# Second-norm tiles turned in the router's PSUM bank; first-norm tiles keep the turn bank

## What is computed

```python
y = einsum('nsi,oi->nso', patchify(x), tok_W) + tok_b
h = layernorm(y) * ln_w + ln_b
# attention: first norm, then q, k, v; all fake-quantised
a = norm(h)
q, k, v = split(a @ Wqkv.T)                  # 12 heads of 16, clipped to -4..3
p = quant(q @ k.T / 196)                    # clipped to 8 levels from 0 up, no softmax
h = h + quant(p @ v) @ Wproj.T + bproj
# experts: second norm, then router and experts
f = norm(h)
logits = (f @ enc_w + enc_b) @ sw_w + sw_b   # 8 experts
prob = max(softmax(logits)); onehot = one_hot(argmax(logits))
g = gelu(f @ w1[e] + b1[e]) for the chosen e
out = h + prob * (g @ w2[e] + b2[e])
```

## Time and profile before

| | us |
|---|---|
| median of 3 runs | 1179.12 |
| lowest, highest | 1174.66, 1179.33 |
| the profiled execution | 1175.08 |
| its span in the trace | 1173.3 |
| TensorE busy | 1064.0 (91%) |
| TensorE weight loads | 865.9 (74%) |
| VectorE busy | 864.6 (74%) |
| ScalarE busy | 702.7 (60%) |
| GpSimd busy | 619.2 (53%) |

### The profile page before, as it was taken

How to read it: one execution, slowest core, us unless ns; L and a number is a source line. 1 busy time by engine, 2 the same in 40 slices (tenths; PEclk the granted TensorE clock), 3 DMA queues, 4 the chain that set the end, 5 groups by cost and what they waited for, 6 DMA issues and landing times. The chain is left out here.

```text
span 1173.3 us, 26470 instructions
## 1 busy us (share of the span) xinstructions
PE 1064.0 (91%) x8646; PEld 865.9 (74%) x8646; DVE 864.6 (74%) x2976; ACT 702.7 (60%) x1586; POOL 619.2 (53%) x1016
## 2 busy tenths in 40 slices
PE   4788998999999999999999999999999999999987
PEld 4566777877778777777877777787777778777666
DVE  4587677777877878787777778777777877878673
ACT  1356656665675657666665666666666666666551
POOL 3444563737556373755627366462746646374433
PEclk8887999999999999999999999999999999999889
DMA  7120111111111111111112021121202111000000
GB/s 229 36 60 24 49 53 41 51 32 51 43 44 56 42 50 34 51 40 41 59 34 60 23 63 40 40 60 34 60 22 63 40 39 60 10 11 13 8 16 22
DMA packets 33517, 52.80 MB, mean 45 GB/s; under 512 B 5077, under 2 KB 18150, under 8 KB 33382
## 3 DMA queue, kind: packets, MB, share of 16 engines
q1 hardware_dynamic: 33382, 51.10, 14.8%
HBM read 41.45 MB, written 9.63 MB: 44 GB/s over the span
## 5 line engine op out<-in xcount | busy, mean ns | idle before, releaser
L829 ACT ACTIVATE relu<-scores_ps,c_prob 98x784 uint8<-98x784 f32 x384 | 348.5, 908 | 108.6 <-PE scores_ps L624 83.2
L553 PE MATMUL embed_ps<-we,x_sb 128*112 128x192 f32 x1344 | 303.2, 340 | 22.5 <-ACT y L798 13.7
L912 POOL TENSOR_TENSOR ve<-mv,const_sb 112x1 f32<-112x1 f32 x336 | 74.1, 221 | 375.4 <-DVE mv L1274 373.7
L915 POOL TENSOR_TENSOR rs<-ve,const_sb 112x1 f32<-112x1 f32 x336 | 224.8, 669 | 26.5
L553 PEld LDWEIGHTS embed_ps<-we,x_sb 128*112 128x112 f32 x1344 | 208.1, 180 | 38.5 <-issue 17.0
L1119 DVE TENSOR_SCALAR prob<-relu 98x784 uint8<-98x784 uint8 x384 | 219.4, 572 | 13.1 <-ACT relu L829 4.9
L925 POOL TENSOR_TENSOR expd<-econst,below 112x8 f32<-112x8 f32 x112 | 190.8, 1743 | 25.3 <-DVE below L1197 25.3
L1080 DVE TENSOR_SCALAR xn<-h,mv,rs 112x192 f32<-112x192 f32 x224 | 93.7, 424 | 46.6 <-POOL rs L915 44.8
L930 POOL TENSOR_TENSOR m<-n,lnw 112x192 f32<-112x192 f32 x112 | 67.1, 599 | 105.0 <-ACT n L806 104.8
L819 ACT ACTIVATE a_hi<-turn_ps 128x112 fp32r<-128x112 f32 x112 | 29.5, 264 | 141.7 <-PE turn_ps L571 141.0
L570 PE MATMUL turn_ps<-const_sb,xn 112*128 112x112 f32 x224 | 69.3, 309 | 45.1 <-DVE xn L1080 24.2
(11 more groups left out here) (168 smaller groups left out, 2528.7 us busy)
## 6 DMA issues: line engine op xcount, KB each, us to landing
x_sb<-in_x SPq DMA_DIRECT2D x112, 336.0 KB, 2.9
out<-out_sb SPq DMA_DIRECT2D x112, 84.0 KB, 1.7
we<-in_tok_w SPq DMA_DIRECT2D x1, 576.0 KB, 3.9
w_sb<-in_w SPq DMA_DIRECT2D x1, 384.0 KB, 4.4
const_sb<-in_const SPq DMA_DIRECT2D x1, 377.0 KB
raw_q_a<-in_w_qkv SPq DMA_DIRECT2D x1, 288.0 KB
raw_q_b<-in_w_qkv SPq DMA_DIRECT2D x2, 144.0 KB
raw_a<-in_w SPq DMA_DIRECT2D x1, 256.0 KB, 4.3
```

The source lines that it names most:

```text
L553: pe.matmul(dst, x_sb[:, t, j], we[:, j], start=j == 0, stop=False)
L829: act.activation(relu8[:, u % 2], scores_ps[0:KEYS, :, 0:2 * SEQ], ACT.Relu, scale=c_prob[0:KEYS, :]).then_inc(act_relu, 1)
L912: pool.tensor_tensor(ve[:, t], mv[:, t, 1:2], const_sb[0:TT, C_EPS:C_EPS + 1], ALU.add).then_inc(ve_sem, 1)
L915: pool.tensor_tensor(rs[:, t], ve[:, t], const_sb[0:TT, C_HALFNEG:C_HALFNEG + 1], ALU.pow).then_inc(rs_sem, 1)
```

## The change

Second-norm tiles are turned into `route_ps` instead of `turn_ps`; `turn_bank(k)` picks the bank in `turn`, `high` and `low`. The first-norm turns keep `turn_ps`, and wait only for `low` of the first-norm turn before, in this pass or the last. The second-norm turns become users of the router's bank: `ROUTED` gets seven more entries, which wait with `empty` for the user before and are waited for by the user behind, through `dve_lo`. Since entries are sorted by slot, fractions give the order inside a slot as TensorE runs it: turn +0.1, `up` +0 or +0.3 (`up_place`), `route` +0.4, spread +0.5. No instruction is added, dropped or moved in any engine's order.

```diff
--- before.py
+++ after.py
@@ -382,6 +382,10 @@
             TURNS += [(1, t) for t in at(TURN2, s)] + [(2, t) for t in at(TURN3, s)]
             TURNS += [(3, t) for t in at(TURN3, s + SLOTS)]
 
+        def up_place(slot):
+
+            return slot if slot <= EMBED_END[-1] else slot + 0.3
+
         class Turns:
 
 
@@ -414,9 +418,10 @@
         PROJECTED = [(s, 2, dve_h1, NT, t + 1) for t, s in enumerate(PROJ) if s < SLOTS]
         PROJECTED += [(s - SLOTS, 3, dve_h1, NT, t + 1) for t, s in enumerate(PROJ) if s >= SLOTS]
         PROJECTED += [(s, 3, result, NT, t + 1) for t, s in enumerate(DOWN) if t % 2 == 0]
-        ROUTED = [(s, 3, choose, CHOICES, STEPS_A_CHOICE * n + 2) for n, s in enumerate(ROUTE)]
-        ROUTED += [(s, 3, spread_out, 2, n + 1) for n, s in enumerate(SPREAD)]
-        ROUTED += [(s, 3, gelu_out, 8, n + 1) for n, s in enumerate(UP) if n % 2]
+        ROUTED = [(s + 0.4, 3, choose, CHOICES, STEPS_A_CHOICE * n + 2) for n, s in enumerate(ROUTE)]
+        ROUTED += [(s + 0.5, 3, spread_out, 2, n + 1) for n, s in enumerate(SPREAD)]
+        ROUTED += [(up_place(s), 3, gelu_out, 8, n + 1) for n, s in enumerate(UP) if n % 2]
+        ROUTED += [(TURN3[t] % SLOTS + 0.1, k, dve_lo, None, n) for n, (k, t) in enumerate(TURNS) if k != 1]
 
         def empty(eng, users, groups, slot):
 
@@ -433,8 +438,13 @@
                     if isinstance(loop, int) and number < 0:
                         return
                 _, stage, signal, per_group, k = users[n]
+                if groups[stage - 1] is not None and signal is dve_lo:
+                    return wait(eng, dve_lo, turns.before(groups, k + 1))
                 if groups[stage - 1] is not None:
                     return wait(eng, signal, groups[stage - 1].count(per_group, k))
+
+        def turn_bank(k):
+            return turn_ps if k == 1 else route_ps
 
         block = ctx.enter_context(nc.Block())
 
@@ -565,10 +575,17 @@
                 src, made = (xn2, dve_xn2) if k == 1 else (xn3, dve_xn3)
 
                 pe.wait_ge(made, g.count(NT, t + 1))
-                wait(pe, dve_lo, turns.before(groups, n))
+                if k == 1:
+                    m = max(range(n - len(TURNS), n), key=lambda m: (TURNS[m][0] == 1, m))
+                    i = g.offset - (m < 0)
+                    if i >= 0:
+                        wait(pe, dve_lo, turns.before(stages(g.loop, i, i % 2), m % len(TURNS) + 1))
+                else:
+                    empty(pe, ROUTED, groups, TURN3[t] % SLOTS + 0.1)
+                bank = turn_bank(k)
                 rows = src[:, (g.parity + t) % 2]
-                pe.transpose(turn_ps[:, 0:TT], rows[:, 0:128], ident)
-                pe.transpose(turn_ps[0:LO, TT:2 * TT], rows[:, 128:EMBED], ident).then_inc(turned, 1)
+                pe.transpose(bank[:, 0:TT], rows[:, 0:128], ident)
+                pe.transpose(bank[0:LO, TT:2 * TT], rows[:, 128:EMBED], ident).then_inc(turned, 1)
 
             def rows(g, m, half):
 
@@ -661,7 +678,7 @@
                 last.then_inc(projected, 1)
 
             def route(groups, g, part):
-                empty(pe, ROUTED, groups, ROUTE[part])
+                empty(pe, ROUTED, groups, ROUTE[part] + 0.4)
                 need_split3(g, PARTS[part][-1] + 1)
                 for n, t in enumerate(PARTS[part]):
                     cols = slice(TT * t, TT * (t + 1))
@@ -692,7 +709,7 @@
             def up(groups, g, n):
                 part, m = divmod(n, FC)
                 bank, users = (wide_ps, WIDE) if n % 2 == 0 else (route_ps, ROUTED)
-                empty(pe, users, groups, UP[n])
+                empty(pe, users, groups, UP[n] if n % 2 == 0 else up_place(UP[n]))
                 if m == 0:
 
                     pe.wait_ge(spread_out, g.count(2, part + 1))
@@ -816,10 +833,10 @@
                 act.wait_ge(turned, turns.before(groups, n) + 1)
                 if t == 0:
                     reads_done(act, g, k)
-                act.activation(hi[:, g.parity, cols], turn_ps[:, 0:TT], ACT.Copy)
-                last = act.activation(both[0:LO, g.parity, cols], turn_ps[0:LO, TT:2 * TT], ACT.Copy)
+                act.activation(hi[:, g.parity, cols], turn_bank(k)[:, 0:TT], ACT.Copy)
+                last = act.activation(both[0:LO, g.parity, cols], turn_bank(k)[0:LO, TT:2 * TT], ACT.Copy)
                 if k != 1:
-                    last = act.activation(f_c[0:LO, g.parity, cols], turn_ps[0:LO, TT:2 * TT], ACT.Copy)
+                    last = act.activation(f_c[0:LO, g.parity, cols], turn_bank(k)[0:LO, TT:2 * TT], ACT.Copy)
                 last.then_inc(act_hi, 1)
 
             def relu(g, u):
@@ -1106,9 +1123,9 @@
                 hi, lo, both = (a_hi, a_lo, a_b) if k == 1 else (f_hi, f_lo, f_b)
                 cols = slice(TT * t, TT * (t + 1))
                 dve.wait_ge(act_hi, turns.before(groups, n) + 1)
-                dve.tensor_tensor(lo[:, g.parity, cols], turn_ps[:, 0:TT],
+                dve.tensor_tensor(lo[:, g.parity, cols], turn_bank(k)[:, 0:TT],
                                   hi[:, g.parity, cols].bitcast(f32), ALU.subtract)
-                dve.tensor_tensor(both[LO:128, g.parity, cols], turn_ps[0:LO, TT:2 * TT],
+                dve.tensor_tensor(both[LO:128, g.parity, cols], turn_bank(k)[0:LO, TT:2 * TT],
                                   both[0:LO, g.parity, cols].bitcast(f32), ALU.subtract).then_inc(dve_lo, 1)
 
             def quantise(g, u):
```

## The result

The changed kernel takes 1254.93 us as the median of four runs (1253.94 to 1256.71), against 1177.7 us for the kernel before, now with a fourth run of it (1174.66 to 1179.33). The ratio is 1.066, with a 95% interval of 1.063 to 1.069. The direction was right; the time lies 10 us above the forecast range.

A forecast was written before the change was run, and what follows sets the result against it. TensorE, busy 91% of the span in one fixed order, was taken to bound the kernel. 1175.1 profiled + 39.7 for stalls less gain + 13 for the clock = 1227.8, stated as 1228 us, range 1205 to 1245.

The forecast's parts named there:

- The removed waits: Slots 21 and 23: first-norm turns no longer wait for f_b, 18.3 us in all, 1.21 us a pass.
- The two stalls: New TensorE waits: router in slot 2 for tile 4, 2.30 us; expert product in slot 9 for tile 6, 1.32.
- the gain: Slots 21 and 23: idle time saved at first-norm turns, 0.33 + 0.88 = 1.21 us a pass.
- the sum: Steady passes without the clock: 2.30 + 1.32 - 1.21 = 2.41 us each; with passes 1, 16 and 17, +39.7 us.
- the third case: Slot 2's stall mostly swallowed because VectorE sets slots 4 to 6: 1195 us, chance 0.08.
- the three falls of the one before: Clock falls to half in passes 3, 8 and 13, slots 21 to 22, of the kernel before; 1.3 us each.
- The clock: Behind slot 2: half-clock falls in some 13 of 14 steady passes, where 3 had one; 10 x 1.3 = +13 us.
- The case with two stretches a pass: Two half-clock stretches each pass, at slots 2 and 9 or one that lasts: +36 us, 1251 us, chance 0.07.

The follow-up runs named there:

- the kernel with tiles 0 to 3: Changed kernel, but only second-norm tiles 0 to 3 use the router's bank; tiles 4, 5, 6 return to the turn bank: 1161.96 us, ratio 0.990.
- the kernel with tile 4 back: Changed kernel with tile 4 alone returned to the turn bank, removing the router's wait in slot 2: 1184.09 us, ratio 1.008.
- the one with slot 2 filled: Changed kernel plus ten unread products, 448 columns wide, ahead of the router's wait in slot 2: 1224.13 us, ratio 1.042.
- the kernel with all waits filled: Changed kernel plus unread wide products ahead of three waits: ten in slot 2, six in slot 9, four in slot 20: 1210.73 us median, 1206.66 profiled.
- with narrow products: Changed kernel plus twenty unread products, 16 columns wide, ahead of the router's wait in slot 2: 1259.05 us, ratio 1.072.
- with tile 6 back: Changed kernel with tile 6 alone returned to the turn bank, removing the expert product's wait in slot 9: 1237.56 us, ratio 1.054.
- with the wait alone: Kernel before, no tile changing bank, with only the router's wait in slot 2 moved from tile 3 to tile 4: 1266.25 us, ratio 1.078.

## Why the prediction was wrong, point by point

**The removed waits** were right: 18.3 us gone from the list, 1.1 to 1.3 us a pass by the kernel with tiles 0 to 3.

**The two stalls** were right in place, cause and nearly in size. The router started 488.33 - 488.28 = 0.05 us after the read ended instead of the 0.14 taken, and slot 2 costs about 2.1 us a pass (68.8 to 70.9, the kernel with tile 4 back against the one with slot 2 filled) instead of 2.30, and slot 9 1.2 instead of 1.32. The list shows only 1.93 us of idle time in slot 2, and 30.2 in all instead of 37, because idle time counts from the end of the embedding product ahead; the 2.30 was the delay of the router's start, which the prediction called idle. Together with the gain a steady pass without falls is 2.2 us longer, where the sum had 2.41. That both carry through nearly whole was right as well: the third case, a stall swallowed by slot 6, did not come, and the turns still wait 19.4 + 5.1 = 24.5 us for `xn`, against 24.2 before. Without the clock the forecast had +39.7; the kernel with all waits filled is 1206.7 - 1175.1 = 31.6 above the profiled kernel before, or 35.5 if the three falls of the one before, 3.9 us, are taken off it.

**The clock** is the step that failed: a term of 13 us that came to about 43. The loss in the profiled executions is 78.9 us, of which the stalls less the gain make 14 x 2.2 = 30.8 in the steady passes and 4.8 in the last two. (The changed kernel is 1253.9 - 1206.7 = 47 us above the one with all waits filled, but that one also lacks falls that the kernel before had.) The falls did come, where they were expected and from the cause named. Three things in the term were too small:
- *How long.* I took one stretch of 3.4 us a pass. The changed kernel has none in pass 2, and in the 13 passes after it stays down 3.4, 6.8 or 10.2 us, as these windows of passes 3, 4 and 11 show; that is 23 stretches of 3.4 us against 13.

```profile
186.70:260.80 74.10, 68.03 (x541) 55.30 (x542) 52.93 (x184) 43.95 (x100) 38.60 (x64) 0.95 0.15 42
260.80:333.40 72.60, 66.57 (x541) 53.94 (x542) 52.94 (x184) 44.00 (x100) 38.58 (x64) 0.98 0.15 43
...
773.30:848.70 75.40, 69.52 (x541) 56.42 (x542) 52.88 (x184) 43.86 (x99) 38.55 (x64) 0.93 0.14 41
```

- *What one costs.* Against 70.9 with the clock up these passes lose 1.7, 3.2 and 4.5 us, so 1.5 to 1.7 for each 3.4 us. The 1.3 came from falls at slot 21. A likely reason, not tested, is that TensorE waits for others there anyway and that behind slot 2 its queue is full. In all, the steady passes are 1028.8 - 14 x 70.9 = 36 us longer than without a fall (31 against the kernel with all waits filled).
- *Where.* The last two passes had no clock term. They went from 90.8 to 107.4 us; 4.8 of that are the stalls (95.6 with all waits filled, where 7 was forecast), and 12 the clock, as far as one execution of each can part them.

The case with two stretches a pass, 1251, was the nearest. I had its price of 40 us at hand, gave it 0.07, and ended the range at 1245, below it. The prediction gave no reason against it. Nothing in the rows said that a fall behind a thin stretch must be a single one, and pass 16 of the kernel before already had a long one: right behind the half clock of the earlier trace rows stands

```profile
1093.50:1100.30 6.80, 6.57 (x41) 5.20 (x42) 4.40 (x13) 2.46 (x3) 2.75 (x6) 0.50 0.00 0
```

The rule of thumb of the Trainium skill (TensorE: Matmul & The Clock Gate, "HAM oscillation") warns only of idle gaps longer than these. Here it is not enough: 1.93 us of idle time with narrow products behind it brought the clock down in 13 of 14 passes. What the Trainium skill says of small idle times on the same page ("A second HAM failure mode: psum-queue depth-cycling") agrees with the falls behind 0.9 us in slot 20.

## What to carry to other kernels

Before giving a busy bank a new user, list the order of its users in time and ask of each who now stands right behind the new one: a user that arrives while the slowest reader of the new tile is still queued behind other work pays that reader's whole delay. Here tiles 0 to 3 fit into the router's bank for nothing and tiles 4 and 6 did not (tile 5 was not tried by itself), and the choice was a list of four numbers. Price a wait on a full TensorE with the clock that may fall behind it: look for what runs next, and where that is narrow too, reckon with a multiple of the wait.

## What the runs showed of the hardware

- A TensorE wait of 2.0 us a pass, 31.6 us in all, cost 91 us, nearly three times itself, with nothing else changed.
- Products 16 columns wide did not hold the clock up: TensorE issuing them without a gap for 2.4 us gave 1259 us (7.2% above the kernel before on its chip), idle 1255 (6.6%), products 448 columns wide 1224 (4.2%).
- Four products that nobody reads, in an idle 0.9 us, made a kernel faster by 11 us (1162.0 to 1151.0). They kept TensorE at 2.4 GHz in all 14 steady passes, where six had fallen to 1.2 GHz, and this is 6.7 us of it in the profiled executions.
- Whether a fall comes, and for how long, differs from pass to pass of the same program (3.4, 6.8, 10.2 us), though the waits are the same to 0.01 us. The length goes with how late the clock falls after the start of the router's first product in slot 2. In the changed kernel it stays down 6.8 us where it falls at -0.02 to 0.31 us from that start (six passes), 10.2 us at 0.42 and 0.53 (two), and 3.4 us at 1.06 to 1.35 (five). The kernels with narrow products, with tile 6 back and with the wait alone fall into the same three groups, with the bounds between 0.35 and 0.42 us and between 0.81 and 0.88 us. What sets the moment of the fall was not tried.
